# Two attention and expert layers on one core: a new order of the written-out steps, with other transfers first

## The reference, cut to what matters

```python
x = x + _L0_xattn_ref(_layernorm(x), ctx_2048, mask)     # scores, mask, softmax, times the context
x = x + _L0_ffn_ref(_layernorm(x), Wr, Wg, Wu, Wd)       # the best 2 of 8 experts for each row
x = x + _L1_xattn_ref(_layernorm(x), W_qkv, W_o, ..., ctx_2048, ctx_2048, 54)  # only the 54 largest scores
x = x + _L1_ffn_ref(_layernorm(x), w1, w2)               # rows and weights rounded to integers, gelu
```

## Time and profile before

| what | value |
|---|---|
| median of 3 executions | 411.09 us (410.61 to 411.27) |
| the profiled execution | 412.79 us |
| its span, first to last instruction | 410.7 us |
| TensorE busy | 356.3 us, 87% of the span |
| VectorE busy | 291.6 us, 71% |
| ScalarE busy | 189.4 us, 46% |
| moved by transfers | 76.41 MB, 186 GB/s on average |

### The profile page before, as it was taken

How to read it: one execution, slowest core, us unless ns; L and a number is a source line. 1 busy time by engine, 2 the same in 40 slices (tenths; PEclk the granted TensorE clock), 3 DMA queues, 4 the chain that set the end, 5 groups by cost and what they waited for, 6 DMA issues and landing times. The chain is left out here.

```text
span 410.7 us, 6718 instructions
## 1 busy us (share of the span) xinstructions
PE 356.3 (87%) x2108; PEld 284.7 (69%) x2114; DVE 291.6 (71%) x713; ACT 189.4 (46%) x344; POOL 59.2 (14%) x136
## 2 busy tenths in 40 slices
...
PEclk9999999999999999999999999999999696686999
...
GB/s 231 380 286 43 248 375 140 288 183 205 287 301 296 272 273 95 77 141 269 266 315 299 260 308 263 214 102 81 285 60 109 13 95 28 1 161 71 53 14 53
DMA packets 70811, 76.41 MB, mean 186 GB/s; under 512 B 5356, under 2 KB 69496, under 8 KB 70776
## 3 DMA queue, kind: packets, MB, share of 16 engines
...
q0 software_dynamic: 1536, 4.20, 3.1%
...
## 5 line engine op out<-in xcount | busy, mean ns | idle before, releaser
L995 PE MATMUL GU<-xgT,wg_ring 128*128 128x128 f32 x480 | 58.8, 277 | 4.4 <-issue 4.0
L995 PEld LDWEIGHTS GU<-xgT,wg_ring 128*128 128x128 f32 x480 | 56.4, 192 | 8.4 <-issue 6.4
L677 ACT ACTIVATE pT<-T 128x512 f32<-128x512 f32 (+1 forms) x64 | 31.8, 511 | 50.8 <-PE T L931 46.9
L948 PE MATMUL A<-pT,v_sb 128*128 128x128 f32 (+1 forms) x416 | 54.9, 290 | 0.0
L948 PEld LDWEIGHTS A<-pT,v_sb 128*128 128x128 f32 (+1 forms) x416 | 53.7, 207 | 1.4 <-issue 0.3
L1278 DVE MAX8 cand_h<-fold 128x8 f32<-128x801 f32 x56 | 54.4, 981 | 0.0
L917 PE MATMUL S<-k_sb,xT 128*128 128x400 f32 (+2 forms) x128 | 50.9, 538 | 1.4 <-ACT xT L662 0.8
L917 PE MATMUL S<-k_sb,qT 128*128 128x400 f32 (+2 forms) x128 | 48.3, 513 | 2.8 <-ACT qT L735 1.6
L944 PE MATMUL A<-v_sb,pT 128*128 128x256 f32 (+1 forms) x208 | 48.9, 380 | 0.0
L931 PE MATMUL T<-ident,row 128*128 128x128 f32 (+1 forms) x208 | 34.8, 298 | 14.8 <-DVE row L1314 8.3
L1290 DVE MATCH_REPLACE8 fold<-cand_h,fold 128x801 f32<-128x801 f32 x48 | 46.8, 976 | 0.0
...
## 6 DMA issues: line engine op xcount, KB each, us to landing
v_sb<-ctx SPq DMA_DIRECT2D x36, 512.0 KB, 4.9
...
k_sb<-ctxT SPq DMA_DIRECT2D x16, 400.0 KB, 4.9
...
```

The source lines that it names most:

```text
L677: act.activation(pT[0:r, i % NPT, :, :].rearrange("p a s -> p (a s)")[:, 0:w], t_bank("pT", *key)[0:r, 0:w], ACT.Copy).then_inc(pTe_done, 1)
L948: mm = pe.matmul(A_bank[:, o * P:(o + 1) * P], v[0:r, a, o * P:(o + 1) * P], pT[0:r, j, a, :], start=m == 0 and o == 0, stop=m == NMC - 1 ...
L995: mm = pe.matmul(gu_bank(*key)[:, a * F + f * P:a * F + (f + 1) * P], wg_ring[:, w % NWG, a, k, f * P:(f + 1) * P], cols[:, k, :], start=k ...
```

## The change

Only the string `ORDER` changes; it has the same 1439 steps, and all code that reads it is the same, one line further down (L917 becomes L918). Nearly every line of the string differs. In the new list:

- `ldx.0` is followed by the four chunks of keys of batch 0; `ldx.1`, `ldx.2`, `ldx.3` stand between and behind the first two units of values. Before, `ldx.2`, `ldx.3` and `ldx.1` stood ahead of the second chunk of keys.
- `fixed` stands behind the keys of batches 1 and 2, right behind `zero` and `ldv.3.0.1`.
- `wload.1` stands behind `exp1.1`; `wload.2`, `wqa.2`, `wqs.2` and `wqb.2` come later too.
- From there on all engines have another order of the same steps.

```diff
 ORDER = """
-ldx.0 stats.1.0 ldx.2 ldx.3 ldk.1.0.1 ldx.1 ldk.1.0.2 ldk.1.0.0 ldk.1.0.3 aggr.1.0 var.1.0 rstd.1.0 stats.1.2 wload.1
...
+ldx.0 stats.1.0 aggr.1.0 var.1.0 rstd.1.0 norm.1.0 xT.1.0 xTe.1.0 ldk.1.0.3 ldk.1.0.1 s1.0.1 ldk.1.0.2 s1.0.2 mask.0
+ldk.1.0.0 ldx.1 ldv.1.0.0 ldx.2 stats.1.1 s1e.0.1 ldv.1.0.1 ldx.3 s1.0.0 s1e.0.2 s1e.0.0 s1.0.3 aggr.1.1 var.1.1
+s1.1.2 s1e.0.3 rstd.1.1 max1.0 norm.1.1 stats.1.2 stats.1.3 aggr.1.2 ldv.1.0.3 ldv.1.0.2 s1e.1.2 s1.1.1 s1e.1.1 exp1.0
...
```

More of the change, by code:

```diff
@@ L77 @@
[L77 to L86, removed]
@@ L122 @@
-mul.1.4 s3.3.1 maxH.1.4 xgl.1.10 ye.1.3 yst.1.3 thr.0 down.1.5 maxL.1.2 xgT.1.7 xgT.1.8 ye.1.5 ldk.3.2.0 exp3.0
-xgl.1.9 down.1.4 GU.1.6 repH.1.4 wd.1.7 repL.1.2 wg.1.8 wd.1.8 xgTe.1.7 maxH.1.5 xgTe.1.8 cut.0.0 GU.1.7 pT.3.0.0
-silu.1.6 mul.1.6 silu.1.7 xgl.1.11 yst.1.5 pairH.2 ye.1.4 mul.1.7 xgT.1.10 down.1.6 maxL.1.3 pTe.3.0.0 maxH.2.0 GU.1.8
-ye.1.6 xgTe.1.10 repH.1.5 wg.1.9 wd.1.9 nmax.2 pairL.2 silu.1.8 repH.2.0 down.1.7 xgT.1.9 mul.1.8 pvm.3.0.0 wg.1.10
-xgTe.1.9 pT.3.0.1 ye.1.7 maxH.2.1 maxH.1.6 pT.3.0.2 wd.1.10 maxL.2.0 down.1.8 repH.2.1 yst.1.4 wg.1.11 repL.2.0
@@ new lines @@
+pTe.1.2.0 s1.3.0 x1.1 s1.3.3 s1e.3.0 ldv.1.1.1 pT.1.2.1 stats.2.0 aggr.2.0 wqs.1 s1e.3.3 ldk.1.2.3 xT.1.2 xTe.1.2
+pvm.1.2.0 pTe.1.2.1 wqb.1 mask.2 ldk.1.2.0 ldv.1.1.2 pT.1.2.2 ldv.1.1.3 zero ldv.3.0.1 fixed pT.1.2.3 s1.4.1 pTe.1.2.3
+var.2.0 max1.3 rstd.2.0 s1.4.2 exp1.3 wload.2 r1.1 pTe.1.2.2 pvm.1.2.1 s1e.4.1 pvm.1.2.2 s1e.4.2 norm.2.0 pT.1.3.0
+pTe.1.3.0 pvm.1.2.3 pT.1.3.1 pTe.1.3.1 s1.4.0 pT.1.3.2 s1e.4.0 s1.4.3 x1.2 pvm.1.3.0 s1e.4.3 pTe.1.3.2 max1.4 pT.1.3.3
+pTe.1.3.3 xT.2.0 pvm.1.3.1 ldv.1.2.0 wqa.2 coef_e exp1.4 ldk.3.0.3 pvm.1.3.2 ldv.1.2.1 pvm.1.3.3 s1.5.3 x1.3 norm.1.3
```

181 lines of the change are left out of this document (95 added, 86 removed).

## The result

| | before | the change |
|---|---|---|
| median | 411.18 us (410.61 to 411.88, 4 executions) | 416.58 us (413.43 to 419.3, 4 executions) |
| ratio, 95% interval | | 1.0114 [1.0058, 1.0171] |
| the same in a later comparison | 411.42 us (23 executions) | 416.53 us (6), ratio 1.0116 [1.0074, 1.0158] |
| the profiled execution, its span | 412.79, 410.7 us | 414.72, 412.6 us |

A forecast was written before the change was run, and what follows sets the result against it. TensorE was taken to bound the kernel until 178 us, VectorE from there until shortly before the end. The terms -0.7 + 1.3 + 0.4 + 0.5 - 0.1 made +1.4 us, a median of 412.5 us, range 408.7 to 416.0.

The forecast's parts named there:

- the likeliest case: Whole kernel: slower than before by more than 0.2%, chance 0.48, against 0.28 for faster and 0.24 for within 0.2%.
- w2's rival: Near 66 us: w2 lands late, at 67.5, costing 2.5 us behind ScalarE's `wqa.2`; 415.0 us, chance 0.09.
- Place 1: The start: no wait for keys, earlier clock rise, 1.7 us idle ahead of `s1.1.0`; -0.7 us, bounds -2.3 and +1.0.
- the assumption that the clock's rise moves with the work: Start: TensorE works without a gap from 9.10, so its clock rises 3.6 us earlier, at 14.6.
- the rule that the prediction set against this term: Start: hardware checks TensorE's activity on its own rhythm, so the rise need not move; anything between -0.7 and +1.0.
- The cover of `fixed`: Ahead of `exp1.4`: `zero` and `fixed` cost nothing while TensorE has 16 us of work behind them.
- Place 2: Fourth load of rows: TensorE waits 1.3 us for xg ahead of the fourth `xgT`; +1.3 us, bounds 0 and +4.2.
- Place 3: Second group's first blocks: the `mul` wait grows by 0.9, `pos.1` stands 0.7 earlier; +0.4 us, bounds -0.7 and +1.1.
- Place 4: Second group's gathers: VectorE waits 1.9 us for the second gather instead of 1.38; +0.5 us, bounds -1.4 and +2.3.
- Place 5: Smaller ones: the wait ahead of `gabs.2.0` goes, `wo.7` near the end may wait more; -0.1 us, bounds -0.7 and +0.6.

The follow-up runs named there:

- h3: The change's order up to ahead of its `upd.4.0`, the kernel before's order behind it; 415.88 us, ratio to before 1.0103.
- c1: The change with three SyncE loads (`ldv.3.3.0`, `ldv.3.2.2`, `ldk.3.2.1`) put behind `ldv.3.3.1`; 413.75 us, ratio to before 1.0042.
- a2: The change as it is, measured and traced a second time; ratio to before 1.0116.
- h1: The kernel before with the 551 steps ahead of its first `pairH.0` in the change's order; 414.83 us, ratio 1.0035.
- b1: The kernel before with two loads (`ldk.3.2.2`, `ldv.3.2.2`) put behind `ldv.3.2.3`; 411.05 us, ratio 1.0004.
- b2: The kernel before with one load more (`ldv.3.3.0`) among the gathers, ahead of `ldv.3.2.3`; 413.86 us, ratio 1.0043.
- h2: The 551 steps ahead of `pairH.0` as in the kernel before, the rest in the change's order; 415.15 us, ratio 1.0082.
- h4: The kernel before up to its first `pairH.0`, then the change's order with three loads put later; 411.81 us, ratio 1.0034.
- e1: The change with VectorE's norm and statistics behind `s1e.1.2` and `s1e.1.1`, and `coef_e` behind `exp1.4`; 413.67 us, ratio to before 1.0093.
- s1: The kernel before with only the 77 steps ahead of `pT.1.1.0` in the change's order; 425.02 us, ratio 1.0327.

## Why the prediction was right, and where not

The sign was right: slower, the likeliest case. The size was not: +1.4 us against +4.7. The ratio on the median of 411.09 gives 415.8, just inside the range's end of 416.0; the median itself, 416.58, is outside by 0.6 us. That the range reached so far was luck: its end stood on w2's rival, which did not happen, and by the text's own numbers (w2 there at 67.5, wanted at 66.5) that rival was 1 us late, not 2.5.

*Place 1, the start, -0.7: gone.* The waits came as written: none for keys, then `s1.1.0` behind VectorE's norm and statistics, 0.96 us instead of 1.7. Against before's own execution the place gave -2.06, but that execution started 2.1 us late; against the list's usual start it gives +0.2. What failed is the assumption that the clock's rise moves with the work. TensorE begins at 9.10 and works without a gap in every trace of the new start; the first pass at the faster spacing starts at 12.5 (h3), 13.0 (the change), 13.1 (c1), 14.4 (a2) and 14.5 us (h1), and with the old start at about 13 (b1), 13.8 (b2), 15.1 (h2) and 18.3 (before). By the rule that the prediction set against this term (the Trainium skill, "TensorE: Matmul & The Clock Gate", "What's actually happening"), the rise follows a rhythm of the hardware's own. These runs agree.

*The cover of `fixed`, at nothing: failed.* The text called the scalars harmless because they were wanted only at `coef_e`; it did not cost SP's queue, where they stand behind the zero fill. +1.0 us up to `GU.0.0`: 78.12 to 78.53 in four traces, against 77.19 to 77.20. The gap of TensorE ahead of `pT.1.4.0` is 0.55 to 0.83 us of it; the rest stays open. In h1, with the same steps, `coef_e` waited 1.20 us, TensorE did not wait, and `GU.0.0` came 77.29 us behind `pT.1.0.0`. The rival with w2 had the right engines and steps, but the wrong transfer: `wqa.2` began at 64.92 without a wait for w2, `log_tau` was late. In its place 0.76 us was lost, not 2.5.

*Place 2, +1.3: nothing.* The row landed in time, although all landings are as before, 3.9 at the median. From `GU.0.0` to `pairH.0` the change's four traces with this list have 76.45 to 78.03, before's first four 76.55 to 77.21 (h1 has 77.89, and h4, with before's list, its unexplained 80.94).

*Place 3, +0.4:* the waits grew by 0.9, as the working had it.

*Place 4, +0.5, bound +2.3: the term that was too small.* The two updates of tile 4 waited 0.96 + 3.32 = 4.28 us instead of 1.38: +2.9, above the bound (3.36 us and +2.0 in the second trace). The text priced the wait for the second gather alone; the long wait, 3.32 us, is for the fourth, for which it had no term. It noted that two loads of values stood behind `upd` steps now, and took this for less traffic. A place in the list behind a VectorE step holds nothing back on SP, which waits only for its own semaphores: the loads were issued at once, five in 3 us. And the text followed the late row only to the update. Behind it came TensorE's 4.87 us of idle, the clock at 0.74 and 2.2 us at `pairL.4`. With the three loads moved (c1_loads_later) all of this was gone: `upd.4.1` and `pairL.4` did not wait, and the ratio fell from 1.0116 to 1.0042. From `x3.0` to `thr.3` VectorE's idle was 6.48 us, and 5.22 in the second trace, against 1.38.

*Place 5, -0.1:* the wait ahead of `gabs.2.0` was gone in the first trace and 0.93 us in the second; `x3.7` waited 1.27.

By medians of the traces: +0.2 at the start, +1.0 up to `GU.0.0`, +0.3 up to `pairH.0`, and +3.4 from there to `thr.7` (208.8 for the change, a2, h2 and e1; 205.4 for before, b1 and s1; 205.6 if h1, 208.22, is taken in), +0.3 behind it: 5.2, where the ratio says 4.7. The +0.2, +0.3 and +0.3 are each smaller than the differences between traces of one list.
